# PSUM banks in pairs, one exponential and one maximum for two heads, and a new placing of the jobs in the attention windows

## What is computed

```python
# layer 0, a batch is an image; L = 32 latent channels
score = softmax(einsum('bcn,bcm->bnm', th, ph)); lat = einsum('bnm,bcm->bnc', score, g)
sa_out = gamma_sa * conv1x1(lat, w_o) + x        # then attention to 128 concepts, added too
# layer 1: class map, its norm, a small gate, added to x
# layer 2: group norm, 8 heads of 32 channels
q, k, v = split(einsum('oc,bct->bot', w_qkv, group_norm(x)) + b_qkv)
weight = softmax(einsum('bct,bcs->bts', q * scale, k * scale))      # 1024 x 1024 for each head
h = einsum('oc,bct->bot', w_proj, einsum('bts,bcs->bct', weight, v)) + b_proj
x = x + h
# layer 3: group norm, qkv, at every token a softmax over the 8 x 8 products of its heads, projection, added to x
```

## Time and profile before

| | |
|---|---|
| median of 3 runs | 1921.55 us (1916.68 to 1927.38) |
| the profiled execution, whole | 1920.26 us |
| its span, first to last instruction | 1918.5 us |
| mean granted TensorE clock | 0.940 of full |
| busy: TensorE, VectorE, ScalarE, GpSimd | 89%, 72%, 41%, 71% |
| windows 0 and 1 (layer 0), and layer 1 | about 52 to 340 us |
| the 8 iterations of layer 2 | about 343 to 1475 us |
| layer 3's own part | about 1475 to 1918 us |

### The profile page before, as it was taken

The page is one execution under the profiler, slowest core; times in us unless marked ns, Lnnn a source line. Parts: engine busy times, 40 slices in busy tenths (PEclk is TensorE's granted clock), DMA queues, the critical chain, the costliest instruction groups (busy, mean ns, idle before and its releaser), DMA issues.

```text
span 1918.5 us, 37187 instructions
## 1 busy us (share of the span) xinstructions
PE 1702.5 (89%) x15160; PEld 773.6 (40%) x15160; DVE 1374.5 (72%) x2153; ACT 787.1 (41%) x1546; POOL 1357.7 (71%) x581
## 2 busy tenths in 40 slices
PE   5897765799999999999999999999997678889974
PEld 2332222344344444344344344444442345555541
DVE  5677567887777877767867877777771158878875
ACT  0352401155455555455455455455555233333320
POOL 0573600088788887887888878878789059989996
PEclk8898887799999999999999999999998889999986
DMA  5000030220001001001001010010010211222211
GB/s 189 1 2 1 2 129 0 84 77 23 2 2 67 2 2 67 2 9 60 2 24 45 2 59 11 1 67 2 2 45 1 89 29 55 88 77 75 74 51 47
DMA packets 48432, 75.11 MB, mean 39 GB/s; under 512 B 30804, under 2 KB 31110, under 8 KB 48262
## 3 DMA queue, kind: packets, MB, share of 16 engines
q1 hardware_dynamic: 38758, 72.15, 10.6%
q10 hardware_dynamic: 9504, 0.59, 0.3%
HBM read 44.87 MB, written 25.17 MB: 37 GB/s over the span
## 4 chain that ended last, share of the span: by engine, by line
PE 77%; DVE 13%; issue 3%; ACT 2%; DMA 2%; POOL 1%; SPq 1%; POOLq 0%; DVEq 0%; ACTq 0%
PE AV L652 14%; DVE MX L1292 7%; PE S L626 6%; PE RB L895 6%; PE S L688 4%; PE S L603 3%; PE AV L908 3%; PE RB L626 3%; PE RB L944 3%; PE S L638 2%; PE RB L603 2%; PE S L630 2%; PE S L678 2%; PE RB L688 2%; PE S L634 2%
## 5 line engine op out<-in xcount | busy, mean ns | idle before, releaser
L1201 POOL TENSOR_TENSOR ACC<-ACC,PR 128x1024 f32<-128x1024 f32 x360 | 840.9, 2373 | 34.4 <-ACT PR L1034 34.4
L1034 ACT ACTIVATE PR<-S 128x512 f32<-128x512 f32 x667 | 358.6, 603 | 373.1 <-PE S L638 242.9
L1292 DVE TENSOR_REDUCE MX<-S 128x1 f32<-128x512 f32 x646 | 409.4, 681 | 124.2 <-PE RB L603 60.5
L1201 POOL TENSOR_TENSOR ACC<-PR 128x1024 f32<-128x1024 f32 x72 | 168.9, 2368 | 343.0 <-ACT PR L1034 131.6
L652 PE MATMUL AV<-PR,VT 128*32 128x512 f32 x2304 | 312.9, 616 | 3.8 <-ACT PR L1034 3.3
L1292 DVE TENSOR_REDUCE MX<-RB 128x1 f32<-128x512 f32 x336 | 218.5, 681 | 73.8 <-PE S L603 57.0
L1034 ACT ACTIVATE PR<-RB 128x512 f32<-128x512 f32 x328 | 183.7, 604 | 168.9 <-PE S L638 63.4
L626 PE MATMUL S<-HI 32*128 32x512 f32 x667 | 195.6, 493 | 6.2 <-DVE NMR L1305 2.5
L1227 POOL TENSOR_TENSOR PR<-WO,WRK 128x1792 f32<-128x1792 f32 x32 | 155.6, 4883 | 27.9 <-DMA WO<-WO 12.9
L1227 POOL TENSOR_TENSOR PR<-WO,VT 128x1792 f32<-128x1792 f32 x32 | 155.0, 4867 | 10.3 <-DMA WO<-WO 8.3
L603 PE MATMUL S<-HI 32*128 32x512 f32 x646 | 156.2, 507 | 3.4 <-ACT PR L1034 2.8
(11 more groups left out here) (357 smaller groups left out, 3250.9 us busy)
## 6 DMA issues: line engine op xcount, KB each, us to landing
X<-out_y SPq DMA_DIRECT2D x24, 1024.0 KB, 5.0
out_y<-X SPq DMA_DIRECT2D x16, 1024.0 KB, 4.9
X<-in_x SPq DMA_DIRECT2D x8, 1024.0 KB, 8.5
OHU<-out_y SPq DMA_DIRECT2D x8, 512.0 KB, 4.4
X<-out_y SPq DMA_DIRECT2D x8, 512.0 KB, 4.1
out_y<-X SPq DMA_DIRECT2D x8, 512.0 KB, 3.1
out_y<-OHU SPq DMA_DIRECT2D x8, 512.0 KB, 3.1
WO<-WO SPq DMA_DIRECT2D x128, 16.0 KB, 1.9
```

Source lines behind the costliest of these rows:

```text
L1034: nc.scalar.activation(exps(s, pair)[:, HALF * one:HALF * one + HALF], RING[ring.place()], ACT.Exp, scale=1.0 if i is None else float(D) * ...
L1201: nc.gpsimd.tensor_tensor(ACC[:, pair, :], so_far, exps(s, pair), ALU.add).then_inc(pool_used, 1)
L1292: nc.vector.tensor_reduce(out=MX[:, h, t, keys:keys + 1], in_=bank(), op=ALU.max, axis=AX.X).then_inc(ring_free, 1)
```

## The change

- The ring has three places, each a pair of neighbouring banks: two of `S4`, two more of `S4`, the two of `RB`. A pair holds two heads of the scores or two heads of the maxima. The seventh bank, `SUM`, is outside the ring (`Single`): the jobs qk, v, post, spread, gn and sums in the windows take it by turns. `flip` takes a pair (of which it uses one bank). `concepts`, `turn`, `classes`, `norms` and `write` of layers 0 and 1 take pairs.
- ScalarE makes the exponentials of two heads in one instruction of 128 x 1024, and VectorE the maxima of two heads in one instruction, 128 x 2 x 512 to 128 x 2; semaphores `exp_done`, `st_full` and, for maxima, `ring_full` and `ring_free` count pairs.
- A v job makes four key tiles with 16 matmuls (was two with 8), so a window has two v jobs.
- Maxima go through the queries' tiles for the first half of the keys, then for the second. They wait for the count of the split that they need, no longer for `stage_ready`.
- Jobs beside the maxima, per step of a middle image's windows. First window before: 1 sums, qk; 2 qk; 3 qk; 4 post; 6 spread, post; 7 flip, v; 9 sums, v, v; 10 v; 11 qk; 12 post, gn; 14 spread; 15 flip, post. After: 0 qk; 1 sums; 2 qk; 3 post; 4 v; 5 post; 6 spread; 7 flip, v; 8 qk; 9 sums; 10 qk; 11 gn; 12 post; 14 spread; 15 flip, post. Second window before: 1 sums, qk; 2 qk; 3 qk; 4 v; 6 spread, v; 7 flip, v; 9 sums; 10 v; 11, 12 stats; 13 gn; 14 spread; 15 flip, qk. After: 0 qk; 1 sums; 2 qk; 3 v; 6 spread; 7 flip, v; 8 qk; 9 sums; 10 qk; 11, 12 stats; 13 gn; 14 spread; 15 flip. Steps 1 and 9 have two tiles of maxima, steps 7 and 15 none, all others one.

The diff, cut to its core:

```diff
-EXPS = H * STEPS
-SLOTS = 7
+EXPS = 2 * STEPS
+SLOTS = 3
...
-        self.at, self.slots = 0, tuple(range(SLOTS))
+        self.at = 0
     def place(self):
         self.at += 1
-        return self.slots[(self.at - 1) % len(self.slots)]
+        return (self.at - 1) % SLOTS
     def skip(self, n):
         self.at += n
-    def align(self, to=0):
-        while self.at % SLOTS != to:
+    def align(self):
+        while self.at % SLOTS:
             self.at += 1
-    def only(self, slot):
-        self.at, self.slots = 0, (slot,)
-
-
-def places(job, single):
-
-    if job[0] == "v":
-        return 2 if single else 1
-    return {"max": 4, "stats": 0, "negate": 0, "reread": 0, "concepts": 4, "softmax": 0, "turn": 4,
-            "classes": 2, "norms": 2, "pool": 0, "regate": 0, "write": 4}.get(job[0], 1)
+
+class Single:
+
+
+    def __init__(self, banks):
+        self.n, self.banks = 0, banks
+
+    def bank(self):
+        return self.banks[self.n]
+
+    def last(self):
+        self.n = 1
+
+
+def places(job):
+
+    return {"max": 2, "flip": 1, "concepts": 2, "turn": 2, "classes": 1, "norms": 1, "write": 2}.get(job[0], 0)
...
-QK_ORDER = ((1, 0), (1, 1), (0, 0), (0, 1))
+QK_ORDER = ((1, 0), (0, 0), (1, 1), (0, 1))
 def maxima(half):
-    return [("max", half, t, keys) for t in range(TILES_HALF) for keys in range(2)]
+    return [("max", half, t, keys) for keys in range(2) for t in range(TILES_HALF)]
 def window_jobs(post=False, nxt=True, gn=False, ahead=0, trail=True, single=False):
@@ -124,21 +132,20 @@
             jobs[first + SUM_AT].insert(1, ("sums",))
             jobs[first + SPREAD_AT].append(("spread", half - 1))
     if nxt:
-        for step, job in zip((1, 2, 3, MT + (3 if post or gn or single else 7)), QK_ORDER):
+        for step, job in zip((1, 2, 3, MT + 3) if single else (0, 2, MT, MT + 2), QK_ORDER):
             jobs[step].append(("qk",) + job)
-        parts = (6, MT + 1) if single else (7, MT + 1, MT + 1, MT + 2) if gn else (4, 6, 7, MT + 2)
-        for n, step in enumerate(parts):
+        for n, step in enumerate((6, MT + 1) if single else (4, 7) if gn else (3, 7)):
             jobs[step].append(("v", n))
     if post:
-        for step, job in zip((4, 6, MT + 4, MT + 7), ((0, 0), (1, 0), (0, 1), (1, 1))):
+        for step, job in zip((3, 5, MT + 4, MT + 7), ((0, 0), (1, 0), (0, 1), (1, 1))):
             jobs[step].append(("post",) + job)
     if ahead:
         first = MT + 3 if ahead == 2 else MT
         jobs[first].append(("stats", 0, ahead))
         jobs[first + 1].append(("stats", 1, ahead))
-        jobs[first + 2].append(("gn", 0, ahead))
+        jobs[first + (2 if ahead == 2 else 3)].append(("gn", 0, ahead))
     if gn:
-        jobs[MT + 4].append(("gn", 1, 1))
+        jobs[MT + 5 if ahead else MT + 3].append(("gn", 1, 1))
...
-        RING = [S4[:, n, :] for n in range(4)] + [RB[:, 0, :], RB[:, 1, :], SUM[:, :]]
-        RING_SUM, RING_LAST = 6, 5
+        PAIR = [S4[:, 0:2, :], S4[:, 2:4, :], RB[:, 0:2, :]]
+        SINGLE = (SUM[:, :], RB[:, 1, :])
...
-            def fill(reader, tally, back):
+            def pair(reader, count):
                 slot = ring.place()
                 if slot in held:
                     wait(pe, *held[slot])
-                held[slot] = (reader, tally.now() - back)
-                return RING[slot]
-
-            def bank():
-
-                drained.add()
-                return fill(ring_free, drained, 0)
+                held[slot] = (reader, count)
+                return PAIR[slot]
+
+            def single(reader, count):
+
+                if "single" in held:
+                    wait(pe, *held["single"])
+                held["single"] = (reader, count)
+                return spot.bank()
+
+            def bank(wide=False):
+
+                if wide:
+                    return pair(ring_free, drained.add())[:, 0, :]
+                return single(ring_free, drained.add())
+
+            def banks():
+
+                two = pair(ring_free, drained.add(2))
+                return [two[:, 0, :], two[:, 1, :]]
...
             def max_scores(u, par, half, t, keys):
-                if t == 0 and keys == 0:
-                    wait(pe, stage_ready, 2 * u + half + 1)
+                if t == 0:
+
+                    wait(pe, ring_free, max(kept_qk[u, 0, half], kept_qk[u, 1, keys]))
                 first = HALF * half + P * t
                 for h in range(H):
-                    mm(bank(), HI[par][D * h:D * h + D, 0, first:first + P],
-                       HI[par][D * h:D * h + D, 1, HALF * keys:HALF * keys + HALF],
-                       start=True, stop=True).then_inc(ring_full, 1)
+                    if h % 2 == 0:
+                        dst = pair(ring_free, drained.add())
+                    last = mm(dst[:, h % 2, :], HI[par][D * h:D * h + D, 0, first:first + P],
+                              HI[par][D * h:D * h + D, 1, HALF * keys:HALF * keys + HALF],
+                              start=True, stop=True)
+                    if h % 2:
+                        last.then_inc(ring_full, 1)
...
-                    exped.add()
-                    dst.append(fill(exp_done, exped, 0))
+                    if h % 2 == 0:
+                        two = pair(exp_done, exped.add())
+                    dst.append(two[:, h % 2, :])
...
-                    mm(dst[h], ONER[row, :], NMR[row, half, :], start=False, stop=True,
-                       skip_group_check=True).then_inc(st_full, 1)
+                    last = mm(dst[h], ONER[row, :], NMR[row, half, :], start=False, stop=True,
+                              skip_group_check=True)
+                    if h % 2:
+                        last.then_inc(st_full, 1)
...
-                dst = fill(half_kept, kept, 0)
+                dst = single(half_kept, kept.add(2))
...
-            def v_product(u, part, batch, unit):
-                dst = bank()
+            def v_product(part, unit, wide=False):
+                dst = bank(wide)
                 if part == 0:
                     pe.wait_ge(wv_in, 16)
-                for m in range(2):
-                    mt = 2 * part + m
+                for m in range(4):
+                    mt = 4 * part + m
...
-                    for h in range(H):
-                        pair, one = h // 2, h % 2
-                        wait(act, st_full, EXPS * u + H * s + h + 1)
-                        if one == 0:
-                            prior = s - 4
-                            wait(act, av_done, STEPS * u + prior + 1)
-                            if prior % MT in POOL_TILES:
-                                wait(act, pool_used, 2 * POOL_SUMS * (2 * u + prior // MT)
-                                     + 2 * max(POOL_TILES.index(prior % MT) - 1, 0) + pair + 1)
-                            else:
-                                wait(act, half_done, 2 * u + prior // MT + 1)
-                        nc.scalar.activation(exps(s, pair)[:, HALF * one:HALF * one + HALF],
-                                             RING[ring.place()], ACT.Exp,
+                    for pair in range(2):
+                        wait(act, st_full, EXPS * u + 2 * s + pair + 1)
+                        prior = s - 4
+                        wait(act, av_done, STEPS * u + prior + 1)
+                        if prior % MT in POOL_TILES:
+                            wait(act, pool_used, 2 * POOL_SUMS * (2 * u + prior // MT)
+                                 + 2 * max(POOL_TILES.index(prior % MT) - 1, 0) + pair + 1)
+                        else:
+                            wait(act, half_done, 2 * u + prior // MT + 1)
+                        nc.scalar.activation(exps(s, pair),
+                                             PAIR[ring.place()].rearrange("p a q -> p (a q)"), ACT.Exp,
...
             def row_max(half, t, keys):
-                for h in range(H):
-                    nc.vector.tensor_reduce(out=MX[:, h, t, keys:keys + 1], in_=bank(), op=ALU.max,
-                                            axis=AX.X).then_inc(ring_free, 1)
+                for pair in range(2):
+                    wait(dve, ring_full, drained.add())
+                    nc.vector.tensor_reduce(out=MX[:, 2 * pair:2 * pair + 2, t, keys], in_=PAIR[ring.place()],
+                                            op=ALU.max, axis=AX.X).then_inc(ring_free, 1)
```

129 lines of the change are left out of this document (68 added, 61 removed).

## The result

The changed kernel takes 1967.6 us (median of four runs, 1965.4 to 1974.2) where the kernel before took 1924.4 beside it: ratio 1.0236, 95% interval 1.0194 to 1.0279: slower, clear of no change, by about 2%. The forecast was 1976 us in a range of 1935 to 2020, with a chance of 0.80 for slower. The profiled execution took 1974.2 us (the steps had given 1975.3).

What follows compares the result with a forecast made beforehand. The prediction took TensorE as the only full engine, its scores waiting for VectorE's first reduction to free PSUM. Eight iterations at +6.5 us (+52) and +3 before them gave 1975.3 profiled, 1976 us median, range 1935 to 2020.

Steps and rivals of the forecast that it cites:

- The two-head instructions: A two-head reduction takes 1.21 us, a two-head exponential 1.03; reductions end to end before the iterations gain 2.6 us.
- Wait (a): In steps without a job, the next scores' second pair waits for the first maxima's reduction: 3.93 us instead of 3.40.
- Wait (b): The second maxima wait for the same step's first exponential: 0.17 us later, 2.0 us an iteration over 12 steps.
- (c): In steps with sums and two tiles of maxima, the longer reduction puts the next AV at 6.22 us against 5.79.
- The single bank: Each job waits until VectorE has read the one before; 0.5 us of cover in the latest case, costed at nothing.
- Jobs laid out anew: Table of a middle iteration's steps with the jobs in their new places: 145.4 us against 138.9, +6.5 an iteration.
- The sum: Eight iterations add 52 us and the windows before them 3, taking the profiled execution from 1920.3 to 1975.3 us.
- The early part: Two windows before the iterations: 5.5 us of longer steps less 2.6 gained on reductions, +3, bounds 0 and 6.
- Half clock: Rival, chance 0.23: TensorE's short waits bring more spells at half clock; 2030 us with four more an iteration, 1990 with one.
- Faster: Rival, chance 0.13: the layout pays and pairs cost nothing; an iteration of 135.9 us, 1897 us in all.

## Why the prediction was right, point by point

- **The two-head instructions.** 1.21 us expected, 1.22 measured; 1.03 and 1.02. The line through two lengths of the earlier trace rows held. The gain in the set of reductions on the chain ahead of window 0 was smaller than said: eight pairs take 9.15 us where 16 singles took 9.67, 0.52 us and not 1.3. A tile has four heads, so these 16 reductions are four tiles, and the forecast had counted eight at 0.16 us each; by the tile it is 0.13 us, near what was said. The first AV of window 0 comes only 0.15 us earlier (59.62 instead of 59.77).

```profile
42.68 9.15 DVE MX L1330 x8
```

- **Wait (a).** 3.93 us expected, 3.94 measured in all eleven short steps, the spread's among them. Halving the reduction took 0.53 us off the seven without a spread and 0.3 off three of the four with one, so the cause is shown; what holds the spread steps at 3.62 was not traced. The 0.4 us added for the two steps behind the statistics was wrong: they take 3.94 too, since the wait hides the statistics.
- **Wait (b).** 0.17 us in 12 steps expected; 0.18 in six qk or post steps, two v steps and the four sums steps, which is 12. Halving the exponential took it off all three kinds. The forecast had the count right, but (c) was worked out without the shift.
- **(c), the sums step.** 6.22 expected and 6.42 measured; the 0.2 is (b), which the separate line of the sum held.
- **The single bank.** Costed at nothing, and its jobs waited for no reader. The old placing shows the cost if that cover is gone: 65 us.
- **Jobs laid out anew.** The layout table gave 145.4 us, the trace 144.6; flips take 15.7 instead of 16.3, and the short steps and the v steps each 0.2 less than said. On the ring of seven the same layout gives 140.1 us and saves nothing.
- **The sum.** The iterations were to bring +52 us and brought +40.7. The term that was mis-sized is the iteration of before: 138.9 us was taken, one without a spell at half clock, while four of its six whole iterations had one and their mean is 140.0; that is 9 of the 11 us, and the 0.8 above another 6, against which the first and last iterations cost some 4 more than middle ones. Most of that is the first, counted from AV to AV: 146.1 us against 138.4, at a clock of 0.96 against 0.98. The early part was put at +3 and brought 3.0 up to the last maxima, by other terms than said: the two windows cost 2.4 us more, not 5.5 (their clock reads 0.93 after and 0.89 before), 0.15 was gained ahead of them, and what follows them up to the last maxima took 0.8 more, where the reductions were to gain 2.6 in all. The stage behind it was left out. There the `write` jobs of layer 1 take four banks at a time: four of seven before, four of six after. Their first matmuls, with the idle time before them, before and after:

```profile
357.21 1.19 PE L822 MATMUL S<-VT,WO 32*128 32x512 f32 x1 [2.38 <-DVE MX L1292]
361.73 1.14 PE L822 MATMUL S<-VT,WO 32*128 32x512 f32 x8 [0.85 <-DVE X L1484]
365.15 0.66 PE L822 MATMUL RB<-VT,WO 32*128 32x512 f32 x1 [1.11 <-DVE X L1484]
367.97 0.70 PE L822 MATMUL S<-VT,WO 32*128 32x512 f32 x2 [0.83 <-DVE X L1484]
```
```profile
358.89 2.09 PE L859 MATMUL S<-VT,WO 32*128 32x512 f32 x8 [2.25 <-DVE MX L1330]
364.11 0.70 PE L859 MATMUL RB<-VT,WO 32*128 32x512 f32 x2 [1.42 <-DVE X L1521]
368.73 0.70 PE L859 MATMUL RB<-VT,WO 32*128 32x512 f32 x2 [2.36 <-DVE X L1521]
372.98 1.22 PE L859 MATMUL S<-VT,WO 32*128 32x512 f32 x2 [1.38 <-DVE X L1521]
...
380.90 3.78 PE L718 MATMUL SUM<-X 128*128 128x512 f32 x4
```

  Set follows set after 5.2, 4.6 and 4.3 us instead of 4.5, 3.4 and 2.8: +3.3. From the last set to the first AV it is 5.2 us more, 3.78 of them the qk job that now stands in step 0 and here runs at half clock; from the last maxima to the first set it is 1.3 less. Over the whole stage, from the first set to the first AV, the clock reads 0.68 after and 0.86 before, and TensorE is busy 21.0 us against 15.8. No run took this stage apart, so the split is read from the traces alone, and whether the waits brought the lower clock is not shown.
- **Luck in the total.** The forecast had +55 us between the profiled executions and 53.9 came, but not from its terms. The iterations brought 11.3 less than said; 7.2 in the `write` stage and 3.0 behind the iterations, both put at nothing, filled the place. Each wait was right to 0.03 us and its step count too, so the mechanism stands; that the total fits to 1.1 us is luck.
- **From the profiled execution to the median.** The median was put 1.3 us above the profiled execution; it came out 6.6 below. Against the medians, then, the change costs 43.2 us, and the forecast of 55 was 12 too high.
- **Half clock (0.23).** Didn't come in the middle iterations. TensorE stands still for 0.42 and 0.23 us in the short step above and for 0.85 us in the sums step, and the clock column stays at 1.00 in all six; the spells that the kernel before had in four of six are gone there. In part it did come where layer 2 begins, in the `write` stage and the first iteration (0.68 and 0.96, against 0.86 and 0.98 before). The Trainium skill (TensorE: Matmul & The Clock Gate, A second HAM failure mode: psum-queue depth-cycling) tells of a kernel in which cycling through PSUM banks made the clock swing; this cycling, with a wait in 15 of 32 steps, did not. In the old placing on pairs half clock followed most rests of 1.99 us ahead of a post, and one of six ahead of a v job.
- **Faster (0.13).** Needed a pair at 0.91 us or less. With both waits gone by leaving work out, the iteration is 135.3 us, near the 135.9 of that rival, though with half of the work of two engines left out. What I then expected of the ring of seven (short steps at 3.40 throughout) was not.

## What to carry to other kernels

When several buffers are freed by one wider instruction, what counts is when the first of them comes free, not the busy time saved; how many buffers stay in the ring may count as much, and no run here takes the two apart. Here VectorE and ScalarE were relieved by 4 to 5 us an iteration each and TensorE lost that much. Draw the ring for each kind of step, write down which reader's end each fill waits for, and do so again for every number of places a step takes; the same placing of jobs was worth 9 us an iteration on one ring (144.6 against 153.6) and nothing on the other. Small jobs belong into steps that wait anyway, and what is issued ahead of the work that sets the pace is paid for in the step before.

## What the runs showed of the hardware

- VectorE's reduction across two banks (128 x 2 x 512) takes 1.22 us where one bank takes 0.68; ScalarE's exponential across two takes 1.02 where one takes 0.60. Nothing was added for crossing from one bank to the next. Halved, to 2 x 256, they take 0.69 and 0.60 us, as one bank of 512 does.
- Neighbouring instructions on VectorE start 0.08 us before the length of the one ahead is over, whatever its width (1.14 of 1.22, 0.60 of 0.68), so half as many instructions save half as many fixed parts and no more: 0.07 us for each that goes.
- Rests of 0.2 to 0.9 us, in twelve of the 32 steps by the timeline, left the clock at 1.00. In the kernel before one of 0.73 us was followed by half clock and one of 0.75 us was not the earlier trace rows. Of seven rests of 1.98 to 1.99 us ahead of a post six were followed by it (0.80 us for a first round of scores instead of 0.50), of six ahead of a v job one. So the length of one rest doesn't tell what the clock will do.
